# Two expert layers around attention: sums, weight peaks and norms in one stage, output stored in parts, exponent taken twice

## What is computed

```python
x = L0_attn_x
x = x + 0.5 * _L0_ffn_ref(_layernorm(x), ...)      # block quantized feed forward
x = x + _L0_attn_ref(_layernorm(x), ...)           # selective scan (mamba)
x = x + 0.5 * _L0_ffn_ref(_layernorm(x), ...)
x = x + 0.5 * _L1_ffn_ref(_layernorm(x), ...)      # 16 experts, top 1, capacity 256
x = x + _L1_attn_ref(_layernorm(x), ...)           # attention, 16 heads of 64, causal
x = x + 0.5 * _L1_ffn_ref(_layernorm(x), ...)      # the experts again
return x
```

```python
# experts: each token goes to one expert's buffer, if there is place
buf = zeros((n_exp, cap, d)).at[idx, safe_pos].add(where(keep[:, None], xf, 0.0))
h = relu(einsum('ecd,edh->ech', buf, W1) + b1[:, None, :])
y = einsum('ech,ehd->ecd', h, W2) + b2[:, None, :]
out = where(keep[:, None], y[idx, safe_pos] * gate[:, None], 0.0)

# attention
q, k = (apply_rope(q), apply_rope(k))
dots = where(causal, neg, einsum('bhid,bhjd->bhij', q, k) * scale)
attn = softmax(dots, axis=-1)
out = einsum('bhij,bhjd->bhid', attn, v)
out = relu(out.reshape(b, n, INNER) @ W_o1) @ W_o2      # and a layernorm with gamma
```

## Time and profile before

| | |
|---|---|
| median of 3 runs | 5151.13 us (5150.79 to 5154.98) |
| the profiled execution | 5150.29 us |
| its span, first to last instruction | 5148.7 us |
| mean granted clock of PE | 0.863 of full |
| busy: PE, DVE, ACT, POOL | 3708.2, 3685.3, 2557.9, 2348.4 us |

### The profile page before, as it was taken

How to read it: one execution, slowest core, us unless ns; L and a number is a source line. 1 busy time by engine, 2 the same in 40 slices (tenths; PEclk the granted TensorE clock), 3 DMA queues, 4 the chain that set the end, 5 groups by cost and what they waited for, 6 DMA issues and landing times. The chain is left out here.

```text
span 5148.7 us, 85718 instructions
## 1 busy us (share of the span) xinstructions
PE 3708.2 (72%) x28907; PEld 2589.2 (50%) x28907; DVE 3685.3 (72%) x4478; ACT 2557.9 (50%) x4164; POOL 2348.4 (46%) x1532
## 2 busy tenths in 40 slices
PE   2996645555555569849636898998888888885594
PEld 1663224444444446548613565565555555664483
DVE  6882589999999978820156887888878888875101
ACT  1222466666666622123113676777666666674121
POOL 0220278888888822120214655556656566600202
PEclk9998777777777789959858999999999999996697
DMA  2000001100101100026422222222222222202264
GB/s 84 0 0 5 6 23 31 31 29 29 31 29 31 29 22 0 20 84 193 132 88 57 54 53 47 47 49 69 52 63 52 51 52 55 52 4 90 79 192 132
DMA packets 237294, 276.27 MB, mean 54 GB/s; under 512 B 63771, under 2 KB 185556, under 8 KB 235536
## 3 DMA queue, kind: packets, MB, share of 16 engines
q1 hardware_dynamic: 224032, 244.85, 17.4%
q0 software_dynamic: 8704, 24.35, 1.4%
q10 hardware_dynamic: 4224, 2.76, 0.2%
HBM read 152.60 MB, written 36.04 MB: 37 GB/s over the span
## 5 line engine op out<-in xcount | busy, mean ns | idle before, releaser
L2197 DVE TENSOR_TENSOR att_b_prob_low<-att_b_prob,att_b_prob_high 128x1024 f16<-128x1024 f32 (+2 forms) x640 | 765.5, 1196 | 188.7 <-ACT att_b_prob_high L2158 156.3
L2164 ACT ACTIVATE att_b_prob<-att_b_score,att_soft 128x1024 f32<-128x1024 f32 (+2 forms) x640 | 631.7, 987 | 195.5 <-PE att_b_score L2069 121.5
L2224 DVE TENSOR_REDUCE att_b_neg_max<-att_b_peek 128x1 f32<-128x1024 f32 (+1 forms) x748 | 667.3, 906 | 71.5 <-PE att_b_peek L2046 55.4
L1037 PE MATMUL mix_scan_hT<-ident,mix_scan_h 128*128 128x128 f32 x1024 | 248.7, 390 | 535.1 <-DVE mix_scan_h L985 501.2
L2158 ACT CAST att_b_prob_high<-att_b_prob 128x1024 f16<-128x1024 f32 (+2 forms) x640 | 588.1, 919 | 32.8 <-PE att_b_o L2097 15.5
L2093 PE MATMUL att_b_o<-att_b_vh,att_b_prob_high 128*128 128x65 f16 x4352 | 462.8, 195 | 95.1 <-DVE att_b_heads L2215 54.7
L2093 PEld LDWEIGHTS att_b_o<-att_b_vh,att_b_prob_high 128*128 128x128 f16 x4352 | 399.2, 98 | 217.7 <-DVE att_b_prob_low L2197 129.3
L1037 PEld LDWEIGHTS mix_scan_hT<-ident,mix_scan_h 128*128 128x128 f32 x1024 | 172.1, 197 | 649.4 <-DVE mix_scan_h L985 443.8
L2095 PE MATMUL att_b_o<-att_b_vl,att_b_prob_high 128*128 128x64 f16 x4352 | 460.6, 193 | 0.0
L2097 PE MATMUL att_b_o<-att_b_vh,att_b_prob_low 128*128 128x65 f16 x4352 | 460.4, 194 | 0.0
L2067 PE MATMUL att_b_score<-att_b_q_both,att_b_k_twice 128*128 128x512 f16 (+3 forms) x1280 | 448.2, 350 | 8.9 <-issue 7.3
(11 more groups left out here) (339 smaller groups left out, 9526.5 us busy)
## 6 DMA issues: line engine op xcount, KB each, us to landing
moe_w<-in_L_ffn_W_dram SPq DMA_DIRECT2D x64, 1024.0 KB, 8.0
mix_scan_b_row<-mix_b_rows SPq DMA_DIRECT2D x128, 256.0 KB, 3.2
att_b_crossed<-att_b_raw SPq DMA_DIRECT2D x512, 64.0 KB, 2.0
att_b_q_both<-att_b_halves SPq DMA_DIRECT2D x240, 64.0 KB, 2.0
att_b_k_twice<-att_b_halves SPq DMA_DIRECT2D x240, 64.0 KB, 2.0
moe_slots_in<-moe_route_zero SPq DMA_DIRECT2D x2, 4096.0 KB, 14.3
moe_exp_x<-moe_slots_in SPq DMA_DIRECT2D x32, 256.0 KB, 4.3
moe_slots_out<-moe_exp_y POOLq DMA_DIRECT2D x32, 256.0 KB, 6.6
```

Of the source, the lines that this page charges most:

```text
L1037: last = pe.transpose(hT_ps[:, j * D + m * P:j * D + (m + 1) * P], hs[:, b * W + m * GRP + t * P:b * W + m * GRP + (t + 1) * P], ident[:, :])
L2164: act.activation(prob[:, at:at + width], score[m % 2][:, 0:width], ACT.Exp, scale=soft[:, 0:1])\
L2197: dve.tensor_tensor(prob_low[:, at:at + width], prob[:, at:at + width], prob_high[:, at:at + width], ALU.subtract).then_inc(low_ready, 1)
L2224: last = dve.tensor_reduce(neg_max[:, first + col:first + col + 1], peek_bank(kind, s)[:, base:base + nb * P], AX.X, ALU.max, negate=True)
```

## The change

1. **One stage for sums, peaks and norms.** `moe` no longer ends with `moe_combine` but with a function that it is given. For the first expert layer this is `combine_for_attention`. In its one block POOL issues the 32 gathers in the order of four lots of eight tiles, `ORDER` = (2, 3, 0, 1), so that sequence 1 comes first. SP loads the weights. DVE does the peaks and the powers of two, then, lot by lot, eight sums (`add`), eight statistics, the eight small operations on 8 columns, and eight normed tiles (`normed`). `xn` and the PSUM tiles for turning have four slots, the rest of a tile stands behind the scaled tile of two later, and copy and rest take both chunks of a tile in one instruction. The results of sequence 1 go to buffers of their own and are parked in two parts by SP. The two stages around it are one now.
2. **Output in parts.** For the second expert layer the function is `combine_for_output`: eight parts of four tiles; after the four sums of a part SP stores these tiles to the output, while POOL and DVE go on. `store_x` is gone.
3. **Exponent twice.** `high_part` is gone. `exponents` takes the exponent twice from the score tile, once to `prob` (float32) and once to `prob_high` (float16), and `expd` is counted after the second; the wait for `p_done` stands between them. DVE's `low_part` waits for `expd`.

```diff
...
-def store_x(nc, X, out):
...
-            sp.dma_start(out.rearrange("b (t p) d -> p (b t) d", p=P),
-                         X[:, :].rearrange("p (t d) -> p t d", d=D)).then_inc(x_stored, 16)
-            sp.wait_ge(x_stored, 16)
...
-        moe_combine(nc, X, wide, weight, get, slots_out, name + "_comb")
+        combine(wide, weight, get, slots_out)
...
-def moe_combine(nc, X, wide, weight, get, slots_out, name):
-
-    PARTS = 4
+def combine_for_output(nc, X, out, wide, weight, get, slots_out, name):
+
+    PARTS = 8
+    PART = NT // PARTS
...
+        @block.sync
+        def _(sp):
+            by_tile = out.rearrange("b (t p) d -> p (b t) d", p=P)
+            for i in range(PARTS):
+                sp.wait_ge(added, (i + 1) * PART)
+                sp.dma_start(by_tile[:, i * PART:(i + 1) * PART, :],
+                             X[:, i * PART * D:(i + 1) * PART * D].rearrange("p (t d) -> p t d", d=D)).then_inc(x_stored, 16)
+            sp.wait_ge(x_stored, PARTS * 16)
...
+                    .then_inc(fetched[t // PART], 16)
 
         @block.vector
         def _(dve):
             for i in range(PARTS):
-                dve.wait_ge(fetched[i], NT // PARTS * 16)
-                with dve.Fori(i * NT // PARTS, (i + 1) * NT // PARTS) as t:
-                    dve.scalar_tensor_tensor(out=X[:, rows(t)], in0=wide[:, rows(t)], scalar=weight[:, bass.ds(t, 1)],
+                dve.wait_ge(fetched[i], PART * 16)
+                for t in range(i * PART, (i + 1) * PART):
...
+def experts_and_attention(nc, X, ident, moe_dram, dram, rope, moe_name="moe1", name="att"):
...
-        attention_units(nc, ident, dram, unit, per_unit, soft, name + "_units")
...
-            for b in reversed(range(BATCH)):
-                attention_norm(nc, X, ident, xh, xl, b, f"{name}_in{b}", x_parked if b == 1 else None)
+
+            def combine(wide, weight, get, slots_out):
+                combine_for_attention(nc, X, ident, dram, xh, xl, unit, per_unit, soft, x_parked, wide, weight, get,
+                                      slots_out, name + "_in")
+
+            moe(nc, X, ident, moe_dram, moe_name, combine)
+            acc = inner.enter_context(nc.sbuf_tensor(f"{name}_acc", [P, QT * D], F32))
             attention_heads(nc, ident, dram, rope, xh, xl, unit, per_unit, soft, acc, x_parked, acc_parked, name + "_b")
-        earlier = keep("earlier", [P, QT * D])
+            attention_outputs(nc, X, ident, dram, acc, acc_parked, name)
...
+def combine_for_attention(nc, X, ident, dram, xh, xl, unit, per_unit, soft, x_parked, wide, weight, get, slots_out, name):
+
+    GROUP = 8
+    ORDER = (2, 3, 0, 1)
+    SLOTS_X = 4
...
+            for i in range(2):
+                sp.wait_ge(xl_ready, (i + 1) * GROUP)
+                at = slice(i * GROUP * P, (i + 1) * GROUP * P)
+                for part, x in enumerate((parked_h, parked_l)):
+                    sp.dma_start(by_chunk(x_parked[part])[:, :, at], by_chunk(x[:, :])[:, :, at]).then_inc(stored, 16)
+            sp.wait_ge(stored, 2 * 2 * 16)
+
+        @block.gpsimd
+        def _(pool):
+            for i in range(len(ORDER)):
+                for t in tiles(i):
+                    pool.indirect_dma_start(wide[:, t * D:(t + 1) * D], None, slots_out,
+                                            bass.IndirectOffsetOnAxis(ap=get[:, t:t + 1], axis=0)).then_inc(fetched[i], 16)
...
+            def add(i):
+                dve.wait_ge(fetched[i], GROUP * 16)
+                for t in tiles(i):
+                    dve.scalar_tensor_tensor(out=X[:, rows(t)], in0=wide[:, rows(t)], scalar=weight[:, t:t + 1],
+                                             in1=X[:, rows(t)], op0=ALU.mult, op1=ALU.add).then_inc(added, 1)
+                for u, t in enumerate(tiles(i)):
+                    dve.wait_ge(added, i * GROUP + u + 1)
+                    dve.bn_stats(stats[:, t * 6:(t + 1) * 6], X[:, rows(t)]).then_inc(stats_done, 1)
+                dve.wait_ge(stats_done, 1 + (i + 1) * GROUP)
+                cols = slice(ORDER[i] * GROUP, (ORDER[i] + 1) * GROUP)
+                s6 = stats[:, cols.start * 6:cols.stop * 6].rearrange("p (t s) -> p t s", s=6)
+                of = lambda buf: buf[:, cols]
+                n.link(dve.tensor_tensor(of(diff), s6[:, :, 1], s6[:, :, 4], ALU.subtract))
...
+            def normed(i):
+                cols = slice(ORDER[i] * GROUP, (ORDER[i] + 1) * GROUP)
+                dve.wait_ge(std_ready, i + 1)
+                dve.reciprocal(rstd[:, cols], std[:, cols]).then_inc(rstd_ready, 1)
+                dve.wait_ge(rstd_ready, i + 1)
+                for u, t in enumerate(tiles(i)):
+                    m = i * GROUP + u
+                    make_xn(m, t)
+                    if u >= 2:
+                        make_low(m - 2, t - 2)
+                for u in (GROUP - 2, GROUP - 1):
+                    make_low(i * GROUP + u, ORDER[i] * GROUP + u)
+
+            def make_xn(m, t):
+                b = m % SLOTS_X
+                wait_unless_first(dve, x_turned, m - SLOTS_X + 1)
+                dve.tensor_scalar(xn[:, b * D:(b + 1) * D], X[:, rows(t)], mean[:, t:t + 1], rstd[:, t:t + 1],
+                                  ALU.subtract, ALU.mult).then_inc(xn_ready, 1)
+
+            def make_low(m, t):
+                dve.wait_ge(xh_ready, m + 1)
+                dve.tensor_tensor(place(low, t), by_chunk(xT_ps[m % SLOTS_X][:, 0:D]), place(high, t), ALU.subtract)\
+                    .then_inc(xl_ready, 1)
+
+            add(0)
+            for i in range(len(ORDER)):
+                normed(i)
+                if i + 1 < len(ORDER):
+                    add(i + 1)
+            dve.wait_ge(xl_ready, NT)
...
+            for m in range(NT):
+                b = m % SLOTS_X
+                pe.wait_ge(xn_ready, m + 1)
+                wait_unless_first(pe, xl_ready, m - SLOTS_X + 1)
...
+            act.wait_ge(stats_done, 1)
+            for i in range(len(ORDER)):
+                cols = slice(ORDER[i] * GROUP, (ORDER[i] + 1) * GROUP)
+                act.wait_ge(var_ready, i + 1)
+                act.activation(std[:, cols], var[:, cols], ACT.Sqrt, bias=eps[:, 0:1]).then_inc(std_ready, 1)
+                for u, t in enumerate(tiles(i)):
+                    m = i * GROUP + u
+                    act.wait_ge(x_turned, m + 1)
+                    act.copy(place(high, t), by_chunk(xT_ps[m % SLOTS_X][:, 0:D])).then_inc(xh_ready, 1)
...
             def turn(t, b, kind, done):
                 for v in range(STEPS):
-                    if has_piece(kind, v - 1):
-                        high_part(t, v - 1)
                     if has_piece(kind, v):
                         exponents(t, v)
...
-            def high_part(t, m):
-                at, width = m % 2 * SPAN, width_of(m)
-                act.wait_ge(expd, piece(t, m + 1))
-                wait_unless_first(act, p_done, piece(t, m - 1))
-                act.copy(prob_high[:, at:at + width], prob[:, at:at + width]).then_inc(high_ready, 1)
-
             def exponents(t, m):
                 at, width = m % 2 * SPAN, width_of(m)
                 act.wait_ge(scored, piece(t, m + 1))
                 wait_unless_first(act, low_ready, piece(t, m - 1))
-                act.activation(prob[:, at:at + width], score[m % 2][:, 0:width], ACT.Exp, scale=soft[:, 0:1])\
+                act.activation(prob[:, at:at + width], score[m % 2][:, 0:width], ACT.Exp, scale=soft[:, 0:1])
+                wait_unless_first(act, p_done, piece(t, m - 1))
+                act.activation(prob_high[:, at:at + width], score[m % 2][:, 0:width], ACT.Exp, scale=soft[:, 0:1])\
                     .then_inc(expd, 1)
...
-                dve.wait_ge(high_ready, piece(t, m + 1))
+                dve.wait_ge(expd, piece(t, m + 1))
...
-                  lambda: moe(nc, X, ident, of("L1_ffn_"), "moe1"),
-                  lambda: attention(nc, X, ident, of("L1_attn_"), rope),
-                  lambda: moe(nc, X, ident, of("L1_ffn_"), "moe2"))
+                  lambda: experts_and_attention(nc, X, ident, of("L1_ffn_"), of("L1_attn_"), rope),
+                  lambda: experts_to_output(nc, X, ident, of("L1_ffn_"), out))
         for stage in stages:
             with nc.cleanup_on_exit():
                 stage()
-        store_x(nc, X, out)
```

109 lines of the change are left out of this document (39 added, 70 removed).

## The result

The changed kernel took 5064.89 us (median of 4 runs, 5057.61 to 5068.04) beside 5150.96 (4 runs) of the kernel before: ratio 0.9835, 95% interval 0.9821 to 0.985. The forecast was 5051.7 (range 5012 to 5100). The profiled execution took 5057.61, span 5056.0.

What follows compares the result with a forecast made beforehand. The prediction took latencies to bound the entry, the final store's landing the end, and PE (89% busy) the heads. Savings of 37 + 12.4 + 50 = 99.4 us from 5150.29, plus 0.8 for the median, gave 5051.7 us (range 5012 to 5100).

Steps and rivals of the forecast that it cites:

- Entry: Attention's entry: merging sums, peaks and norms into one stage of four overlapped lots saves 37 us, between 22 and 41.
- S: Start of the new entry stage, 2543.4 us, where the sums started before; the entry's forecast times count from it.
- Rival 3: Entry: POOL's gathers become the bound, the last lot landing at S + 76, 11 us late; total 5063; chance 0.05.
- Output: Program end: storing in eight parts leaves a last landing of 3.2 us and saves 12.4 us, between 9 and 14.
- Exponent twice: Heads: prob_high right behind the first exponent gives DVE and PE their work earlier; 50 us less in all.
- six tenths: Heads: chosen share of PE's 91 us of waits for `heads` and `prob_low` that would go, 55 us.
- The key transfers do not get faster: Heads: projection, crossing, rotation and stacking keep their length, so PE's key wait of 29.6 us grows; 5 us taken off.
- this costs nothing: Heads: score bank held through both exponents is no loss; tightest case leaves 1.52 us for a second exponent of 1.11.
- Rival 1: Heads: DVE becomes the bound, waits for maxima may grow, heads gain only 15 us; total 5087; chance 0.17.
- Rival 2: Heads: all PE's waits behind DVE go, maxima come earlier too; gain 100 us and more; total 5002; chance 0.12.
- Rival 4: Heads: side copies behind the second exponent delay rotation and keys, 15 us over 14 turns; total 5067; chance 0.07.
- Rival 5: Heads: DVE's `prob_low` and POOL's rotation block each other; no gain at a 1.93 us mean, 5210 at 2.1; chance 0.04.

Runs made afterwards that it cites:

- run 8: The kernel before with only the exponent taken twice, entry and output as before; 5126.52 us, ratio 0.9949.
- run 5: The changed kernel with the second exponent, still read from the score bank, at the cast's old place behind the side job's copy; 5100.72 us, ratio 0.9909.
- run 1: The changed kernel with the exponent's part undone: one exponent, then the cast of prob behind the side job; 5081.16 us, ratio 0.9883.
- run 4: The changed kernel itself again, without edits, on the chip of other follow-ups; 5059.36 us, ratio 0.9841.
- run 2: The changed kernel with prob_high cast from prob instead of a second exponent, but right behind the exponent, ahead of the side copy; 5063.85 us, ratio 0.9853.
- run 11: The kernel before, with PE's peeks of the first head waiting for that head's two key copies alone; 5110.22 us, ratio 0.9953.
- run 9: The changed kernel with DVE making the sixth of each turn's eight rotations and POOL the other seven; 5010.99 us, ratio 0.9755.
- run 10: The changed kernel with DVE making each turn's sixth rotation and the exponent's part undone (cast of prob behind the side job); 5072.61 us, ratio 0.988.
- run 6: The changed kernel without the product with the sine in each POOL rotation, so queries and keys differ from the reference; 4939.76 us, ratio 0.9586.
- run 7: The changed kernel with PE's peeks of the first head waiting for that head's two key copies alone, on their own semaphore; 5041.78 us, ratio 0.9788.
- run 3: The changed kernel with the rotation's high half written as a sum of two tiles instead of a copy of the finished sum; 5067.92 us, ratio 0.9851.

## Why the prediction came out as it did

**Entry: 37 forecast, 42.4 measured (35.7 by the traces of runs 8 and 5: 125.6 and 89.9).** The mechanism is as told. The peaks end at S + 17.6 instead of 16.3, since the second reduction waits 1.65 us for its weights instead of 0.31; they come beside the gathers now. A lot takes 14.6 us and not 16.3: eight sums 3.25 (the loop that made them 3.96 is gone), eight statistics 2.70, eight normed tiles 6.6 instead of 7.3. The first has 1.71 us of wait for ACT, 1.28 of it a table load. Rival 3 is out: the gathers have a median of 0.95 us, the last is issued at 2578.9 and has landed by 2581.7, S + 42, for my S + 50.

By the Trainium skill's port rule (SBUF — State Buffer, "Who interferes with whom") as I had worked it out, it would have been S + 60. The trace does not bear that out: of the six gathers issued beside sums two took 1.25 and 1.21 us, the other four and those beside scaled tiles 0.94 or 0.95. I had also read the section too widely. It says that a VectorE instruction with two SBUF inputs contends with a GpSimd instruction that reads SBUF and not with one that only writes it, and infers that writing descriptors needs the write side.

**Output: 12.4 forecast, 14.0 measured.** The last store lands 2.9 us after its issue (5051.97 to 5054.88; median of the eight 3.4, forecast 3.2); the 1 us that I took off for shared transfers was not lost.

**Exponent twice: 50 forecast, 30 measured (22 to 26 by runs 1, 4 and 8).** The first half of the step is right: DVE's wait for ACT fell from 156 to 49 us, PE's waits for `heads` and `prob_low` from 91 to 35.4, 55.7 less where the sum had 55 (six tenths was a choice, so that the two agree so well is luck in part); the maxima gave another 15. Run 2 shows that this is the order's doing. The step that failed is "The key transfers do not get faster ... so the wait of 29.6 grows; I take off 5". It grew by 17.8, and by 42 with the waits called "issue", which I had not counted. The reason stands in that same sentence: the chain from projection over crossing, rotations and stacking to the peek keeps its length, and it ended last in every turn already before (run 11). What PE gains between a turn's first projection and that peek, 22 of 40 pieces, it mostly waits for the keys then: that part of the turn went from 64.4 to 63.3 us only. The 55 us should have been counted for the other 18 pieces alone, by my estimate 55 x 18 / 40 = 25. Runs 9 and 10 show the counterpart: with the chain shortened the exponent's part is worth 54 to 62 us.

A second step failed: "this costs nothing", the room in the score bank. PE's scores wait 18.3 us, in 13 of the 15 turns for 1.25 to 1.26. The timeline of one of them:

```profile
3219.06 0.59 ACT L2185 COPY att_b_raw<-att_b_side 128x512 f32<-128x512 f32 x1 [2.77 <-POOL att_b_halves L1874]
3219.55 1.12 ACT L2207 ACTIVATE att_b_prob<-att_b_score,att_soft 128x1024 f32<-128x1024 f32 x1
3220.55 1.12 ACT L2209 ACTIVATE att_b_prob_high<-att_b_score,att_soft 128x1024 f16<-128x1024 f32 x1
```

```profile
3221.72 0.39 PE L2118 MATMUL att_b_score<-att_b_q_both,att_b_k_twice 128*128 128x512 f16 x1 [1.26 <-ACT att_b_prob_high L2209]
```

The copy waits 2.77 us for POOL to free its half of `raw`, and both exponents and PE's next scores stand behind it. That is POOL's chain again: in run 6 PE's wait for the bank is down to 1.4 us. Taking the bank away from the second reader removed most of it (run 2, 3.3 left), but PE then waited elsewhere (`prob_low` 36.3 instead of 25.9).

**The rivals.** Rival 1 (DVE takes the bound): no, the maxima fell from 43.4 to 28.5, and run 6 shortens the heads by 131 us with DVE's work unchanged. Rival 2: no, though the maxima did improve. Rival 4 gave the right sign and mark (key wait over 45, 5067), but not the cause: the copies are late because POOL has not freed `raw`, not because of the exponent ahead of them; from the second rotation of a turn to the seventh (the peek awaits the keys of the sixth) POOL waited for a copy 0.13 us at most. (The eighth does wait, 0.6 to 4.1 us, but behind that peek.) No run moves the copies themselves. Rival 5: not in its size, the mean of `prob_low` at 1024 columns went from 1365 to 1348 ns. But the narrower ones rose, from 1187 to 1248 ns at 896 columns and from 699 to 832 at 384, and all 640 together took 18 us more; the blocking is real, as told below. (The rival's price for 2.1 us was wrong in itself: 0.17 us more in each of its 640 pieces is 109 us, not 60.) The total came within 13 us of the forecast because the entry and the output gave 7 us more and the heads 20 less.

## What to carry to other kernels

Before you price the waits that an edit removes, look for a chain whose length the edit leaves alone and which ends last once per round, even with a small wait; it takes back what is gained between its two ends, and its waits called "issue" at the same line belong to it. Work on such a chain first: run 7 regroups semaphores and issues nothing new, and gains as much in the heads as the exponent's part. And an engine that is busy for 57% of a stage can be its bound, when its work has to fit between two fixed points of each round.

## What was not expected of the hardware

**POOL's rotations stretch beside DVE.** In a key wait, with DVE idle for 5.9 us, a rotation takes 7.01 us (3130.20 to 3137.21), otherwise 8.6 in the mean. Sorted by what overlaps them in the traces of both kernels, the operations beside no `prob_low` all take their shortest time (the products and the sum 1.25 to 1.28 us, the copy 1.49, the difference 1.15 to 1.16); every longer one, up to 2.46, overlaps a `prob_low`, though not every overlap makes one longer. It works the other way too: a `prob_low` of 1024 columns takes 1.20 to 1.23 us beside no operation of POOL, and in the changed kernel 1.43 in the mean beside one. Shortening one moved the stretching to its neighbours (run 3); leaving one out shortened the rotation by 1.70 us, about its mean of 1.63 (run 6). The Trainium skill (SBUF — State Buffer, "Who interferes with whom") says that a VectorE instruction with both inputs in SBUF contends with a GpSimd one that reads SBUF; `prob_low` is such an instruction, and these rows agree.

**A long wait costs the clock, too.** After 5.38 us of idleness the granted clock was 0.50 for some 4 us of work. The heads' mean clock was 0.98 before, 0.97 after and 0.99 in run 6.

**A stall in the entry.** In runs 5, 6 and 7, which shared a chip, the entry took 89.2 to 89.9 us, in all other traces of the changed entry 78.5 to 78.7. The difference lies in the first lot; the timeline of run 5:

```profile
2577.89 0.37 ACT L1687 CAST att_in_parked_h<-att_in_xT 128x256 f16<-128x256 f32 x1 [4.66 <-issue]
...
2582.79 0.37 ACT L1687 CAST att_in_parked_h<-att_in_xT 128x256 f16<-128x256 f32 x1 [4.53 <-issue]
```

PE, ACT and DVE stand still there in turn while the gathers run, for nothing that the profile shows. What it is stays open.
